# Cross-attention and mixture-of-experts kernel on one core: warm products, gram copy, key centring and the order of the last rows changed

## What is computed

```python
kv  = k_v @ W_k.T + b_k                         # keys, k_v is ctx_512, 128 wide
out = einsum('bij,bjd->bid', p, kv)             # p is the layernorm of x
sim = einsum('bid,bjd->bij', out, kv) * 512**-0.5
sim = (sim - mu) * rsqrt(var + EPS) * ln_gamma + ln_beta
x   = x + softmax(sim)
scores = layernorm(x) @ Wg.T                    # 8 experts
w = softmax of the two best scores
x = x + sum over e of w[e] * (silu(n @ W1[e].T) * (n @ W2[e].T)) @ W3[e].T     # n = layernorm(x)
```

## Time and profile before

| | |
|---|---|
| median of three runs | 388.43 us (388.06 to 389.5) |
| the profiled execution | 388.07 us, of which the span is 386.3 us |
| TensorE busy | 356.9 us (92%), granted clock 0.967 of full on average |
| VectorE busy | 267.9 us (69%) |
| ScalarE busy | 268.2 us (69%) |
| GpSimd busy | 171.6 us (44%) |
| DMA | 57.60 MB, mean 149 GB/s |

### The profile page before, as it was taken

How to read it: one execution, slowest core, us unless ns; L and a number is a source line. 1 busy time by engine, 2 the same in 40 slices (tenths; PEclk the granted TensorE clock), 3 DMA queues, 4 the chain that set the end, 5 groups by cost and what they waited for, 6 DMA issues and landing times.

```text
span 386.3 us, 8154 instructions
## 1 busy us (share of the span) xinstructions
PE 356.9 (92%) x2277; PEld 233.2 (60%) x2277; DVE 267.9 (69%) x661; ACT 268.2 (69%) x467; POOL 171.6 (44%) x202
## 2 busy tenths in 40 slices
PE   5999999998896778889999999999999999999981
PEld 4656676776653545556666666666666666666640
DVE  1268688857976999995757576666767575757660
ACT  1289999979696978976666657575666666666650
POOL 2124856659934135545253434344343435253331
PEclk9999999998776999999999999999999999999997
DMA  6999999999503123255544445353536354544423
GB/s 194 416 383 409 347 382 403 369 317 372 204 3 84 28 57 55 56 86 88 104 66 99 76 91 84 81 90 79 99 66 109 61 106 66 100 73 95 80 30 54
DMA packets 21945, 57.60 MB, mean 149 GB/s; under 512 B 4816, under 2 KB 4944, under 8 KB 20368
## 3 DMA queue, kind: packets, MB, share of 16 engines
q0 software_dynamic: 8736, 20.53, 29.6%
q1 hardware_dynamic: 12016, 30.27, 21.2%
q10 hardware_dynamic: 1152, 6.29, 4.6%
HBM read 38.17 MB, written 18.91 MB: 148 GB/s over the span
## 4 chain that ended last, share of the span: by engine, by line
PE 55%; DVE 6%; issue 4%; DMA 1%; ACT 1%; DVEq 1%; POOLq 0%; ACTq 0%
PE bank L1251 32%; PE bank L1285 17%; PE bank L1242 4%; PE bank L1271 3%; DVE stage L983 2%; DVE Wp L833 2%; DMA out<-kvj_s,sidx 1%; DVE x_s L1015 1%; DVE kvg_s L989 1%; ACT stage L677 1%; DVE n_s L1007 0%; POOLq L74 0%; DVE wsel L999 0%; DVEq L996 0%; DVE wmul L1003 0%
## 5 line engine op out<-in xcount | busy, mean ns | idle before, releaser
L983 DVE SCALAR_TENSOR_TENSOR stage<-W,w3sc,stage 128x512 f16<-128x512 f16 x117 | 84.2, 747 | 6.5 <-ACT stage L677 5.9
L1285 PE MATMUL bank<-stage,n_s 128*128 128x512 f16 (+1 forms) x351 | 82.2, 379 | 3.5 <-DVE n_s L1007 2.0
L1251 PE MATMUL bank<-Wp,kvg_s 128*128 x480 | 80.2, 318 | 4.8 <-DVE kvg_s L989 4.8
L677 ACT ACTIVATE stage<-W,w3sc 128x512 f16 x117 | 80.1, 717 | 0.0
L1251 PE MATMUL bank<-Wp,kv_s 128*128 x456 | 74.3, 313 | 2.0 <-DVE kv_s L989 2.0
L511 POOL DMA_INDIRECT out<-oT_s,sidx x20 | 34.2, 1712 | 75.9 <-ACT oT_s L704 68.7
L1251 PEld LDWEIGHTS bank<-Wp,kvg_s 128*128 128x128 f16 x480 | 47.5, 99 | 32.2 <-issue 6.7
L511 POOL DMA_INDIRECT out<-kvj_s,sidx x19 | 32.4, 1707 | 66.1 <-ACT kvj_s L704 63.5
L1251 PEld LDWEIGHTS bank<-Wp,kv_s 128*128 128x128 f16 x456 | 44.5, 98 | 26.6 <-issue 3.0
L1007 DVE TENSOR_TENSOR n_s<-bank,n_s 128x384 f16<-128x384 f32 x39 | 21.7, 557 | 55.3 <-ACT n_s L690 55.3
L1285 PEld LDWEIGHTS bank<-stage,n_s 128*128 128x128 f16 (+1 forms) x351 | 34.2, 98 | 36.7 <-issue 3.9
(11 more groups left out here) (189 smaller groups left out, 553.8 us busy)
## 6 DMA issues: line engine op xcount, KB each, us to landing
Wp<-in_w SPq DMA_DIRECT2D x8, 1408.0 KB, 11.2
W<-in_w ACTq DMA_DIRECT2D x8, 768.0 KB, 7.6
stage<-in_xT SPq DMA_DIRECT2D x4, 1024.0 KB, 8.2
W<-in_x SPq DMA_DIRECT2D x12, 256.0 KB, 8.6
out<-W SPq DMA_DIRECT2D x12, 256.0 KB, 9.5
n_table<-n_s SPq DMA_DIRECT2D x8, 256.0 KB, 7.6
n_table<-x_s SPq DMA_DIRECT2D x8, 256.0 KB, 6.3
stage<-in_x SPq DMA_DIRECT2D x4, 256.0 KB, 9.2
```

Of the source, the lines that this page charges most:

```text
L677: eng.activation(w3p[t % 2][:, c * D:(c + 1) * D], W3[:, bass.ds(e * W3N + c * D, D)], ACT.Copy, scale=w3sc[:, bass.ds(e, 1)]).then_inc(s_ ...
L983: eng.scalar_tensor_tensor(w3p[r][:, W3N + c * D:W3N + (c + 1) * D], W3[:, bass.ds(e * W3N + c * D, D)], w3sc[:, bass.ds(e, 1)], w3p[r][:, ...
L1251: mm = eng.matmul(bank[2 * which + r][:, 0:H], n_, w_, start=(c == 0 and k == 0), stop=(c == DC - 1 and k == 2))
L1285: mm = eng.matmul(ybank(t - 1)[:, :], h_, w_, start=(c == 0 and k == 0), stop=(c == HC - 1 and k == 2))
```

## The change

- Warm products: 55 instead of 30 at the start, 2 instead of 8 of 128 columns in slots up to 10, 4 instead of 12 of 384 columns in slots 11 to 13, 8 instead of 12 in 14 and 15; 36 instead of 20 after the table; 10 new ones behind turn_rows(0); 3 instead of 6 before the last table group.
- squares(k) takes a whole weight (2816 columns) in every second slot instead of a half in each; the VectorE sum of the two halves and its semaphore go.
- centre_keys(b) one slot sooner on VectorE (for b = 3 slot 7), gram_copy(b) too (slot 9); gram(b) last in TensorE's slot 4(b-1) instead of first in the next. Within the slots the order of the functions stays.
- turned(g) of the odd rows 1 to 11 moves from ScalarE to VectorE, right behind scale_in, with a semaphore of its own.
- The last four rows are sorted in two groups of two (NG = 5 groups in all).
- rank, places, columns, number and table of groups 0 and 1 move ahead: rank(0) to slot 11, places(0) to 12, columns(0) to 13, number(0) to ScalarE's slot 14, table(0) to TensorE's slot 15, and group 1 follows in 14 to 16.
- first_low leaves GpSimd; w12_low(0, 0) does the same on VectorE after the table. w12_high(0, 0) goes from slot 16 to behind turned(15), w12_high(1, 0) ahead of mT_evac(0), turn_rows(0) ahead of the W3 sum.
- The first loads of SyncE go context, W_k, b_k.

```diff
-WARM_GATHER = 20
+WARM_GATHER = 36
+WARM_ROWS = 10
 WARM_DRAIN = 6
-WARM_SLOT = 8
-WARM_LATE = 12
-WARM_START = 30
+WARM_SLOT = 2
+WARM_LATE = 4
+WARM_LAST = 8
+WARM_START = 55
+GROUPS = ((0, 4), (4, 4), (8, 4), (12, 2), (14, 2))
...
+        def by_vector(g):
+            return g % 2 == 1 and g < G - TPB
...
+        def turned_ready(eng, g):
+            if by_vector(g):
+                eng.wait_ge(s_nTv, sum(by_vector(i) for i in range(g + 1)))
+            elif g >= 0:
+                eng.wait_ge(s_nT, sum(not by_vector(i) for i in range(g + 1)))
...
-            eng.dma_start(bk_s[:, :], bk).then_inc(s_bk, 16)
-            for dst, src in ((wk_s[:, :], wkT), (ctx_s[:, 0:N], ctxT[:, 0:N])):
+            for dst, src in ((ctx_s[:, 0:N], ctxT[:, 0:N]), (wk_s[:, :], wkT)):
                 eng.dma_start(dst, src).then_inc(s_key, 16)
+            eng.dma_start(bk_s[:, :], bk).then_inc(s_bk, 16)
...
 (GpSimd)
             router_gap(2)
-            first_low()
             router_weights(0)
...
 (ScalarE, slot)
-                if row(s - 4):
+                if row(s - 4) and not by_vector(s - 4):
                     turned(s - 4)
                 if row(s + 1):
                     scaled(s + 1)
-                if 0 <= s + 3 < 2 * E:
-                    squares((s + 3) // 2, (s + 3) % 2)
+                if (s + 2) % 2 == 0 and 0 <= (s + 2) // 2 < E:
+                    squares((s + 2) // 2)
...
+                if s == 14:
+                    number(0)
                 if s == 16:
-                    w12_high(0, 0)
+                    number(1)
...
             turned(G - 3)
-            number(0)
             turned(G - 2)
             router_exp(0)
             turned(G - 1)
-            number(1)
+            w12_high(0, 0)
+            w3_square(2)
+            number(2)
             w12_high(0, 1)
-            number(2)
-            w3_square(2)
+            number(3)
             w3_square(3)
             router_exp(1)
...
+            w12_high(1, 0)
             mT_evac(0)
-            w12_high(1, 0)
             w12_high(1, 1)
...
 (VectorE, slot)
                 if row(s):
                     scale_in(s)
+                if row(s - 5) and by_vector(s - 5):
+                    turned(s - 5)
...
-                b = batch_at(s, 0, 1)
+                b = batch_at(s, 3, 2)
                 if b is not None:
                     centre_keys(b)
-                b = batch_at(s, 2, 1)
+                b = batch_at(s, 1, 1)
                 if b:
                     gram_copy(b)
...
+                if s == 12:
+                    places(0)
+                if s == 13:
+                    columns(0)
                 if s == 15:
-                    places(0)
+                    places(1)
                 if s == 16:
                     weight_scale()
-                    columns(0)
+                    columns(1)
...
-            places(1)
             chosen(G - 4)
-            columns(1)
             chosen(G - 3)
+            classes(3)
+            class_sums(3)
             places(2)
             chosen(G - 2)
             columns(2)
             chosen(G - 1)
-            classes(3)
-            class_sums(3)
+            classes(4)
+            class_sums(4)
+            places(3)
+            columns(3)
...
             eng.wait_ge(s_et, 1)
-            eng.wait_ge(s_lo, 1)
+            w12_low(0, 0)
             w12_low(0, 1)
             low_rows(0)
...
 (TensorE, slot)
-                b = batch_at(s, 1, 1)
-                if b:
-                    gram(b)
-                b = batch_at(s, 0, 1)
-                if b is not None:
-                    turn_keys(b)
+                first = batch_at(s, 0, 1)
+                if first is not None:
+                    turn_keys(first)
...
                 if row(s - 3):
                     turn_n(s - 3)
+                if first:
+                    gram(first)
                 if s == 13:
                     weight_norms()
+                if s == 15:
+                    table(0)
...
             turn_n(G - 1)
             router(G - 2)
-            table(0)
+            rank(3)
             router(G - 1)
             table(1)
-            rank(3)
+            rank(4)
             counts()
             table(2)
-            warm(wide, WARM_DRAIN)
             table(3)
+            warm(wide, WARM_DRAIN // 2)
+            table(4)
...
+            eng.wait_ge(s_idx, 2)
+            turn_rows(0)
+            warm(oh[:, :, :, :].rearrange("p g k e -> p (g k e)"), WARM_ROWS, 7)
             eng.wait_ge(s_w3q, E)
```

More of the change, by code:

```diff
@@ L293, in ring_free @@
             eng.wait_ge(s_op, B)
-            wait(eng, s_tab, q - 1)
+            wait(eng, s_tab, min(q - 1, 2))
         def ybank(t):
@@ L609, in number @@
                 eng.wait_ge(s_ohp, q + 1)
-                for i in range(TPB):
+                g0, m = GROUPS[q]
+                a = g0 // TPB % 2
+                for i in range(m):
                     cols = slice(i * TOPK, (i + 1) * TOPK)
-                    eng.activation(oh_r[:, q % 2, :, cols], oh_r[:, q % 2, :, cols], ACT.Copy,
-                                   scale=tok1[:, q * TPB + i:q * TPB + i + 1]).then_inc(s_ohn, 1)
+                    eng.activation(oh_r[:, a, :, cols], oh_r[:, a, :, cols], ACT.Copy,
+                                   scale=tok1[:, g0 + i:g0 + i + 1]).then_inc(s_ohn, 1)
             def router_exp(part):
@@ L619, in router_exp, with squares @@
                 eng.activation(edl[:, g0:g1], dlt[:, g0:g1], ACT.Exp).then_inc(s_ed, 1)
-            def squares(k, h):
+            def squares(k):
                 eng.wait_ge(s_w[k], 16)
-                wait(eng, s_wq, 2 * k + h)
-                eng.activation(wjunk, wst[k][:, h * WH:(h + 1) * WH], ACT.Square,
-                               accum_out=wsq[:, k, h:h + 1]).then_inc(s_wq, 1)
+                wait(eng, s_wq, k)
+                eng.activation(wjunk, wst[k], ACT.Square, accum_out=wsq[:, k:k + 1]).then_inc(s_wq, 1)
             def w12_high(k, h):
@@ L936, in then @@
                 eng.wait_ge(s_r, steps[0])
-            places(B - 1)
-            columns(B - 1)
+            places(NG - 1)
+            columns(NG - 1)
             eng.wait_ge(s_cntp, 1)
@@ L1137, in turn_n @@
                 eng.wait_ge(s_n, g + 1)
-                wait(eng, s_nT, g)
+                turned_ready(eng, g - 1)
                 for c in range(DC):
@@ L1179, in slot @@
                 else:
-                    warm(wide, WARM_LATE)
-                if s == 12:
+                    warm(wide, WARM_LATE if s < 14 else WARM_LAST)
+                if s == 11:
                     rank(0)
+                if s == 14:
+                    rank(1)
                 b = batch_at(s, 2, 1)
@@ L1190, in slot @@
                     sims(s + 3)
-                b = batch_at(s, 0, 1)
-                if b is not None:
-                    outs(b)
+                if first is not None:
+                    outs(first)
                 if row(s - 3):
                     turn_n(s - 3)
+                if first:
+                    gram(first)
                 if s == 13:
                     weight_norms()
+                if s == 15:
+                    table(0)
             eng.wait_ge(s_const, 1)
```

80 lines of the change are left out of this document (37 added, 43 removed).

## The result

The changed kernel takes 405.04 us, the median of four runs (399.92 to 409.66), against 388.25 (387.08 to 389.5) for the kernel before, measured beside it. Its two slower runs show the lower clock (0.923 and 0.928 against 0.948 and 0.940), so the ratio is taken from the other two. It is **1.033, interval 1.026 to 1.039**: slower by some 12.6 us. The profiled execution is the one of 409.66 us, so the sizes in its stages are at the upper end; they add up to some 22 us.

The account below looks back on a forecast made before the run. TensorE and ScalarE were taken to bound the row-stage batches, a dependence chain the drain. Terms -1.4 + 1.9 + 3.5 + 1.4 - 2.7 = +2.7 us on a 388.07 us execution; forecast 391.0 us, range 382.5 to 396.

Parts of the forecast that it names:

- two waits: Row stage, VectorE: stands at key centring behind kv_evac and at gram copy behind gram; both add up, 5.2 us in batch 3.
- the start: Up to scaled(3): warm keys(0) and earlier context gain about 2.4 us, 1.7 lost to a centring wait; net -1.4 us.
- rival (a): Row stage: VectorE's spare time hides both waits and the lighter TensorE and ScalarE set the batches; 383 us, chance 0.20.
- batch 2: scaled(3) to scaled(7): VectorE's work, one turned copy and waits of 2.2 and 2.9 us make 18.1 against 16.2, +1.9 us.
- batch 3: scaled(7) to scaled(11): VectorE's work, two turned copies and 5.2 us of waits make 21.0 against 17.45, +3.5 us.
- last rows: scaled(11) to turned(15): early places, columns, number and table(0) make 31.5 us against 30.1, +1.4 us.
- drain: turned(15) to the first tile: without first_low's stall VectorE enters tile 0 at +23.6 against +26.25, -2.7 us.
- centring wait: VectorE at centre_keys, behind ScalarE's kv_evac: 2.4 us in batch 3, 2.2 in batch 2.
- merged square: ScalarE: one square of 2816 columns takes 2.4 us and saves 0.3 against two; by the skill page about 2.5.
- gram wait: VectorE at gram_copy, behind a 7.7 us TensorE chain ending in gram: 2.8 us in batch 3, 2.9 in batch 2.
- Rival (b): Row stage: the waits idle TensorE, its clock falls to half, 1.5 us more in each of three batches; 394.5 us, chance 0.18.
- Fewer warm products: Row stage: 1.3 us a batch off TensorE; with merged squares and turned copies both full engines about 1.2 us a batch faster.

Follow-up runs that it names:

- b_waits: The kernel before with only key centring and gram copy one slot sooner on VectorE: 399.73 us, ratio 1.031.
- a_nowaits: The changed kernel with key centring and gram copy back in their old slots, few warm products kept: 391.59 us, ratio 1.008 to the kernel before.
- a_warm: The changed kernel with the row stage's warm products as before, both moves kept: 403.53 us, ratio 1.043 to the kernel before.
- b_grc: The kernel before with only the gram copy one slot sooner on VectorE: 395.5 us, ratio 1.016.
- a_end: The changed kernel with key centring and gram copy last in their same new slots: 394.4 us, ratio 1.017 to the kernel before.
- n_table: a_nowaits with table(0) out of slot 15, back behind router(14): 388.0 us, ratio 0.999 to the kernel before.
- n_late: n_table with 12 wide warm products again in slots 11 to 15: 388.68 us, ratio 1.000 to the kernel before.
- b_low: The kernel before with only first_low taken from GpSimd and done by VectorE after the table: 386.11 us, ratio 0.994.
- b_fewwarm: The kernel before with only fewer warm products in the slots (2 instead of 8, late 4 and 8 wide instead of 12): 387.44 us, ratio 0.996.

## Why the prediction was right or wrong

**Right: the sign, the two waits and their places.** The forecast was slower, 391.0 us, by two waits on VectorE in the named places, behind kv_evac and behind gram. They are there, with these releasers. b_waits shows that they alone make a loss of 3.1%, and a_nowaits that the rest of the change makes 0.8%. The time lies far outside the range (382.5 to 396); the size failed.

**Which part of the size.** Changes against the kernel before, in us; the forecast without the moves is my estimate from the prediction's sums (the start without its 1.7 us of wait, and the batches as in rival (a)):

| stretch | forecast | change | forecast without the moves | a_nowaits |
|---|---|---|---|---|
| to scaled(3) | -1.4 | -0.2 | -3.1 | -3.2 |
| batch 2, scaled(3) to (7) | +1.9 | +6.2 | -1.0 | +0.4 |
| batch 3, scaled(7) to (11) | +3.5 | +6.6 | -1.2 | +1.1 |
| last rows, to turned(15) | +1.4 | +10.0 | +1.4 | +6.7 |
| drain | -2.7 | -0.4 | -2.7 | -0.6 |

The forecast terms add up to +2.7 us with the moves and to -6.6 without, so the moves were worth 9.3 us in them. The ratios say 9.5 us (13.5 by the medians): near it, but partly by luck, since each of the four waits of batches 2 and 3 was longer than forecast. The larger error is in the rest of the change, forecast -6.6 us and by its ratio of 1.008 +3.3: the last rows first, then the batches and the drain.

**The two waits.** Batch 2 was to be +1.9 and batch 3 +3.5 us; measured +6.2 and +6.6 (in a_warm, at the full clock, +3.3 and +5.7). The centring wait was put at 2.2 to 2.4 us and measured 3.03 twice. Of the excess, 0.14 us is the merged square, longer than my 2.4; most of the rest is scaled, which starts late, as the point after the next shows. The gram wait was put at 2.8 to 2.9 and measured 5.55 and 4.28. The failed step of this term is *"That same copy releases, in TensorE's order, turn_n(4) 0.44, turn_keys(3) 0.44, router(3) 0.8 ..."*: it adds lengths as if TensorE would wait for nothing between them. VectorE's turned(3) and TensorE in batch 3 of the change:

```profile
62.77 0.68 DVE L877 COPY nT_s<-bank 128x512 f32<-128x512 f32 x1
...
63.93 0.60 PE L1162 MATMUL bank<-ident,n_s 128*128 128x128 f32 x4
...
65.81 1.03 PE L1177 MATMUL bank<-wg_s,nT_s 128*128 128x8 f32 x8 [0.84 <-DVE topi L871]
...
71.58 1.06 PE L1128 MATMUL bank<-kvj_s 128*128 128x128 f32 x8
```

From turn_n(4) at 63.93 to the end of gram(3) at 72.64 it is 8.7 us, not 7.7, and 0.84 of the difference is the router's wait for chosen(2), which the centring wait had made late. Another 0.5 us passes between the end of turned(3), from which I counted, and turn_n(4). Together that is the excess of the wait, 4.28 against 2.8. In b_grc, where nothing is late, the same chain is 8.0 us with eight warm products. In batch 2 of this execution the half clock does it:

```profile
41.88 2.04 PE L1155 MATMUL bank<-kvg_s,oT_s 128*128 128x512 f32 x2 [1.23 <-ACT L_s L553]
43.72 5.57 PE L1135 MATMUL bank<-stage,kvj_s 128*128 128x512 f32 x8
```

sims took 2.04 instead of some 1.10 us and outs(2) 5.57 instead of the 3.60 of outs(3): 2.9 us together, about the excess of that wait, behind 1.23 us of idle TensorE. In a_warm, at a clock of 1.00, this wait is 2.67 us, as forecast. I had added two waits as if they were independent; in batch 3 the first feeds the second, by 0.84 us.

**Batch 1.** *"of the 2.4 us some 1.7 go into that wait"* counted only the centring ahead of scaled(0). gram_copy(1) waits too, in slot 1: 3.93 us. That cost isn't in the sum at all. scaled(3) comes at 34.3 us, 0.2 us sooner and not 1.4, and without the moves it comes 3.2 us sooner (31.4). In b_waits, with the old start, scaled(3) is 2.8 us later than before.

**scaled(g) waits for residual(g-2).** I followed only the chain through alpha. The waits of the change have this line, with its eight times, and the timeline has one of them, at scaled(3):

```profile
ACT L_s L553 <- DVE W L859: 6.7, 8, 2.7
```

```profile
34.34 0.69 ACT L553 ACTIVATE L_s<-bank,alpha 128x512 f32<-128x512 f32 x1 [0.86 <-DVE W L859]
```

residual frees the buffer that scaled writes, and stands behind the same waits on VectorE. So ScalarE is stopped at two places, scaled and weigh, and not at one. scaled(3) waited 0.86 us for it and scaled(7) 0.38, and kv_evac stands behind them: that is a good part of what the centring waits are longer than forecast. b_waits shows this wait once, 0.5 us, and a_end, with both steps last in their slots, eight times (6.9 us), so it needs the rest of the change too.

**Rival (b), the clock.** It is real, and of the rivals it was the nearest in size. In the profiled run the granted clock is 0.50 from 80 to 90 us and from 120 to 130:

```profile
80.00:90.00 10.00, 10.00 (x50) 8.18 (x49) 5.26 (x21) 6.49 (x11) 3.73 (x9) 0.50 0.51 187
...
120.00:130.00 10.00, 10.00 (x86) 8.24 (x83) 8.03 (x42) 8.61 (x13) 2.26 (x3) 0.50 0.07 2
```

It may explain scaled(11) to scaled(15), where no moved step waits: 20.3 us at a clock of 0.67, and 17.1 at 1.00 in a_warm. That is only argued: the two are executions of 409.66 and 398.26 us, and without the moves the same stretch was 17.7 us at 0.81 and 17.8 at 1.00 (n_table, n_late). And holding the clock doesn't give the time back: a_warm is 1.5 us faster by the medians (403.53 against 405.04), which four runs each don't tell from nothing. That it would come on top of the waits, and not instead of my forecast, I didn't allow for. The Trainium skill (TensorE: Matmul & The Clock Gate, HAM oscillation) describes such a back and forth between the rates; the clock line of the profile after shows it (9999 6 99 6 5 8 6 5 5).

**Last rows.** *"With table(0) (2.03 us on TensorE) ahead of router(11) I get 31.5 us"*: measured 40.1 us in the change, 36.8 in a_nowaits. This is the largest error, and the failed step is the price of the table: 2.03 us of TensorE's time in a sum that gives +1.4 for all. Taking it out of slot 15 gives 5.3 us back in the trace and 3.6 by the medians, since in a_nowaits the half clock comes again behind it. n_table then has the 31.5 us of the forecast, but without the table that the forecast counted in, so this agreement is partly luck: if the 2.03 us stood in it in full, the other terms of that sum were some 2 us too low. In a_end and a_warm the same stretch, with the table, is 33.0 and 32.5 us. The further 3.3 us of the change over a_nowaits lie in the execution of 409.66 us, at a clock of 0.67 and 0.59.

**The batches without the moves.** Lighter queues on ScalarE and TensorE were to give 1.0 to 1.2 us a batch, and in a_nowaits the batches got longer by 0.4 and 1.1 us. The failed step is *"Taken alone this would speed both full engines"*: it counts busy time and no wait. TensorE is busy for 16.92 of the 18.90 us of batch 3, and the other 1.98 are two waits for VectorE in the old places of the two steps, for the centred keys and for the gram copy:

```profile
54.84 0.66 PE L1121 MATMUL bank<-ident,kv_s 128*128 128x128 f32 x4 [0.95 <-DVE kv_s L734]
...
64.07 1.12 PE L1141 MATMUL bank<-oT_s,G_s 128*128 128x512 f32 x2 [1.03 <-DVE G_s L739]
```

The kernel before has neither wait in this batch: with lighter engines the old places are late, the new ones too early. The merged squares and the turned copies weren't tried alone, so which of them does it stays open.

**The merged square.** Here the page that I cited (the Trainium skill, ScalarE: Activation LUTs, What ACT_TABLE_LOAD costs) was right and my slope of 0.73 ns a column wrong: the trace has 2.54 us for 2816 columns, by its figure 2.5:

```profile
34.93 2.54 ACT L635 ACTIVATE Wp<-Wp 128x2816 bf16<-128x2816 f32 x1
```

**Drain.** -2.7 us forecast, -0.4 measured. gather(0) came at 13.7 us behind turned(15), forecast 13.4, and the long casts are gone; so far right. Two things took it back: mT_evac(0) came at 19.2 instead of 18.2, and then a root of eight numbers on GpSimd, on which ScalarE's first activations wait:

```profile
141.90 1.67 DVE L841 SCALAR_TENSOR_TENSOR Wp<-Wp,wscale 128x1408 f16<-128x1408 f32 x1
142.07 3.03 POOL L510 TENSOR_TENSOR w3rs<-w3sum,half 128x8 f32<-128x8 f32 x1 [2.10 <-DVE w3sum L990]
...
146.19 0.55 ACT L696 ACTIVATE L_s<-bank,winv 128x352 f32<-128x352 f32 x1 [3.65 <-DVE w3sc L994]
```

In b_low the same root begins 0.5 us ahead of the low half and takes 1.66 us. All eight profiled kernels with the order of the change show 3.03 or 3.04 us, all eight with the old order 1.66 or 1.67. In b_low the gain is kept: the drain is 24.1 us, 2.2 less. The failed step of this term is that it follows ScalarE's squares and the weights' store to the first tile and has no price for the root of the W3 sums. The mechanism of moving first_low was right, and its gain was lost to the new order of w12_high(1, 0) and mT_evac(0); that this order is the cause I only argue, since it wasn't tried alone.

**The start** was right in its parts: keys(0) takes 1.08 us instead of 2.05 and ends at 7.89 instead of 9.74 us.

**Fewer warm products** were forecast at about 1.2 us a batch on the two full engines. b_fewwarm gives 1.0 us by the medians and at most 2.7 by its interval, over three batches: 16.4, 17.2 and 15.6 us, where it was 16.4, 17.8 and 16.6.

## What to carry to other kernels

Before a step is moved sooner in the order of an in-order engine, compare the time at which the engine reaches the new place with the time at which the input comes, and follow all that stands behind it, also the buffers and banks that it frees for the engine that makes the next input. Two such waits in one loop needn't be independent: here the first made the second's input late by 0.84 us. Where engines get lighter, count their waits beside their busy time, and don't price a step put into a full queue at its own length: here a table of 2.03 us cost 3.6. A step that must come early goes last in its slot, where these two cost 0.9% instead of 2.4%.

## What the runs showed of the hardware that was not expected

TensorE can show as busy throughout and yet lose its clock. From scaled(15) to turned(15) in a_nowaits, with the table of eight 128x128 f16 products there, and in n_table without it:

```profile
84.76:103.83 19.07, 19.07 (x119) 14.85 (x117) 9.13 (x41) 11.82 (x25) 11.02 (x21) 0.63 0.86 340
```

```profile
84.90:98.70 13.80, 13.80 (x111) 10.77 (x109) 9.03 (x41) 11.70 (x25) 10.62 (x21) 0.75 0.99 391
```

Nearly the same products are 19.07 us at a clock of 0.63 and 13.80 at 0.75. But more clock isn't more speed: n_late, with more warm products, has 1.00 in the same stretch and gains 0.4 us in it and nothing in the whole (388.68 against 388.0 us):

```profile
84.90:98.30 13.40, 11.02 (x111) 8.77 (x108) 8.39 (x41) 11.52 (x25) 10.98 (x21) 1.00 1.00 395
```

And a GpSimd step of eight numbers took 3.03 us when it began within a VectorE pass of 1408 columns and 1.66 when it began 0.5 us ahead of one, as the casts of the earlier trace rows did the other way round.
